# Order of work inside and between the stages of a two-layer language-model tower, on one core

## What is computed

```python
h = tok(x, ...)                                    # embedding rows + position + type, layernorm
h = h + attn0(layernorm(h), Wq, Wk, Wv)            # 32 sequences of 128 tokens, 192 features, causal
h = h + ffn0(layernorm(h), phi, ln_g, ln_b, ...)   # soft mixture: 64 experts x 16 slots, hidden 384
h = h + attn1(layernorm(h), w_qkv, w_proj, b_proj) # 12 heads of 16, rotary tables
h = h + ffn1(layernorm(h), router_w, w1, b1, ...)  # top-1 routing to 8 experts, hidden 768, tanh gelu twice
```

## Time and profile before

| | |
|---|---|
| median of 3 runs | 1349.08 us (1348.38 to 1349.42) |
| the profiled execution | 1348.99 us, span 1347.3 us |
| busy PE / DVE / ACT / POOL | 95% / 73% / 70% / 21% |
| mean granted clock of TensorE | 0.99 of full |

### The profile page before, as it was taken

The page is one execution under the profiler, slowest core; times in us unless marked ns, Lnnn a source line. Parts: engine busy times, 40 slices in busy tenths (PEclk is TensorE's granted clock), DMA queues, the critical chain, the costliest instruction groups (busy, mean ns, idle before and its releaser), DMA issues. The chain is left out here.

```text
span 1347.3 us, 29296 instructions
## 1 busy us (share of the span) xinstructions
PE 1275.2 (95%) x8693; PEld 1139.1 (85%) x8693; DVE 987.0 (73%) x3078; ACT 949.2 (70%) x2393; POOL 286.2 (21%) x317
## 2 busy tenths in 40 slices
PE   8789999999999999999999999799999999969997
PEld 6578888887899998999989998688888888858886
DVE  6988888556787777777777776489999999932331
ACT  2478888888766666666666665288888988845552
POOL 5331110000111111111111110113333233221335
PEclk9999999999999999999999999899999999989999
DMA  6134444447666666666666665655555556315642
GB/s 201 51 136 159 163 167 157 154 179 247 180 199 194 202 191 197 197 194 203 191 195 198 192 203 162 205 148 165 151 167 153 160 161 171 107 40 143 133 97 23
DMA packets 180178, 220.16 MB, mean 163 GB/s; under 512 B 23572, under 2 KB 147002, under 8 KB 180080
## 3 DMA queue, kind: packets, MB, share of 16 engines
q1 hardware_dynamic: 146912, 178.81, 43.6%
q10 hardware_dynamic: 25488, 33.19, 7.3%
q0 software_dynamic: 7680, 6.95, 2.7%
HBM read 141.51 MB, written 79.90 MB: 164 GB/s over the span
## 5 line engine op out<-in xcount | busy, mean ns | idle before, releaser
L1361 PE MATMUL bank<-e_w,e_h_full 128*128 128x192 f32 x1920 | 324.9, 326 | 0.4
L1361 PEld LDWEIGHTS bank<-e_w,e_h_full 128*128 128x128 f32 x1920 | 310.6, 190 | 1.7 <-ACT e_h_full L1442 1.3
L1442 ACT ACTIVATE e_h_full<-bank,e_b 128x512 f32<-128x512 f32 x240 | 165.3, 689 | 154.7 <-PE bank L115 154.7
L1297 POOL TENSOR_TENSOR e_ln_rstd<-e_ln_var_eps,minus_half 128x4 f32<-128x4 f32 x62 | 62.5, 1008 | 436.5 <-DVE e_ln_var_eps L1493 436.5
L1899 ACT ACTIVATE probs<-bank,head_neg_max 128x128 f32<-128x128 f32 x384 | 134.9, 392 | 8.6 <-DVE head_neg_max L2143 7.2
L1500 DVE TENSOR_SCALAR e_rows<-e_slot_sums,e_ln_mean_var,e_ln_rstd 128x192 f32<-128x192 f32 x248 | 77.5, 376 | 77.6 <-POOL e_ln_rstd L1297 77.6
L1403 ACT ACTIVATE e_x_full<-bank,e_ln_shift,e_ln_gain 128x512 f32<-128x512 f32 x124 | 76.5, 667 | 40.9 <-issue 36.6
L1110 PE MATMUL bank<-x,dispatch_weights 128*128 128x193 f32 x512 | 96.0, 329 | 5.9 <-ACT slot_stage L955 4.9
L115 PE MATMUL bank<-e_x_hi,e_w1hi 128*128 128x512 f32 x216 | 95.1, 440 | 4.4 <-DVE e_x_hi_over_lo L109 2.0
L1752 PE MATMUL bank<-slot_outputs_then_w_part,combineT 128*128 128x193 f32 x512 | 94.0, 336 | 1.5 <-ACT combineT L1877 1.5
L1752 PEld LDWEIGHTS bank<-slot_outputs_then_w_part,combineT 128*128 128x128 f32 x512 | 84.7, 192 | 7.7 <-issue 7.2
(11 more groups left out here) (295 smaller groups left out, 3064.5 us busy)
## 6 DMA issues: line engine op xcount, KB each, us to landing
slot_sums<-slot_stage SPq DMA_DIRECT2D x64, 386.0 KB, 3.2
e_slot_sums<-slot_sums SPq DMA_DIRECT2D x64, 386.0 KB, 3.6
slot_outputs<-e_stage ACTq DMA_DIRECT2D x64, 384.0 KB, 3.6
slot_outputs_then_w_part<-slot_outputs SPq DMA_DIRECT2D x30, 768.0 KB, 4.9
e_w<-in_w SPq DMA_DIRECT2D x64, 288.0 KB, 2.9
slot_logits<-kept_logits SPq DMA_DIRECT2D x32, 512.0 KB
slot_logits<-slot_logits SPq DMA_DIRECT2D x32, 512.0 KB, 3.8
e_w1raw<-in_w SPq DMA_DIRECT2D x80, 192.0 KB, 2.7
```

The lines of the kernel that those rows point to most:

```text
L1297: pool.tensor_tensor(rs[u][:], ve[u][:], half[:], ALU.pow).then_inc(rstd_ready, 1)
L1361: last = pe.matmul(y, hf[:, k, js], w2s[u][:, k, :], start=k == 0, stop=k == MT - 1)
L1442: act.activation(hf[:, m, :], hbank(u, m), act_fn, bias=b1s[:, m, ds(n, 1)]).then_inc(acted, 1)
```

## The change

Five parts. (1) Tower: for groups after 3, the first statistics move from slot 0 to slot 6 of the turn before, the mean's subtraction from slot 1 to slot 2, and from group 3 on the type rows are added in slot 5. (2) Combine: the values' product of `q > 0` goes ahead of the transposes of `x4`. (3) Drain: both roundings of the large weights go to the end of ACT's turn 33, both differences to the end of DVE's last turn 36; ACT's router exponentials of turn 33 go behind the batch's own work. (4) Spare products: 6 are added at the start of turn 33, 6 become 2 in turn 34, 4 become 3 ahead of the last head outputs, 20 become 28 at the end, 4 become 7 and 4 become 5 at the seam. (5) Large experts: ACT rounds straight from the banks and DVE subtracts straight from them (no `xf`), the transposes wait for `x_split` in place of `x_taken`; for expert 0 the products of banks 0 and 1 that need only the rounded main part are issued before the split, and the rows of expert 1 are turned after these two banks and taken by ACT after its second gelu.

```diff
@@ tower, DVE
+                AHEAD = 3
                 def embed(e, s):
-                    if s == 0:
+                    if s == 0 and e <= AHEAD:
...
                         norm_stats(e, st6, mv, ve, evar)
-                    if s == 1:
+                    if s == (1 if e <= AHEAD else 2):
                         for j in range(GB):
                             st.did(dve.scalar_tensor_tensor(hrow(e, j), hrow(e, j), mv[:, j, 0:1], T["gamma"][:],
                                                             ALU.subtract, ALU.mult))
+                    if s == 1:
...
-                    if s == 6 and 2 < e + 1 < NG:
+                    if s == (6 if e < AHEAD else 5) and 2 < e + 1 < NG:
                         add_types(e + 1)
+                    if s == 6 and AHEAD < e + 1 < NG:
+                        st.wait_apart()
+                        norm_stats(e + 1, st6, mv, ve, evar)
@@ experts, PE
-                    past(pe, x_taken, 2 * n)
+                    if routed:
+                        past(pe, x_split, n)
+                    else:
+                        past(pe, x_taken, 2 * n)
...
+                        begun = 2 if routed and isinstance(n, int) and n == 0 else 0
+                        pe.wait_ge(w1_split, n + 1)
+                        if begun:
+                            pe.wait_ge(x_hi_ready, 1)
+                            for m in range(begun):
+                                ms = slice(m * P, (m + 1) * P)
+                                pe.matmul(hbank(u, m), w1hi[u][:, 0, ms], xhi[u][:, 0, :], start=True, stop=False)
+                                pe.matmul(hbank(u, m), w1lo[u][:, 0, ms], xhi[u][:, 0, :], start=False, stop=False)
                         pe.wait_ge(x_split, n + 1)
-                        pe.wait_ge(w1_split, n + 1)
-                        for m in range(MT):
+                        for m in range(begun):
...
+                        if begun:
+                            turn_rows(1, 1)
+                        for m in range(begun, MT):
...
-                    keep_busy(pe, T, idle_bank, 4)
+                    keep_busy(pe, T, idle_bank, 7)
                     turn_rows(0, 0)
-                    keep_busy(pe, T, idle_bank, 4)
-                    turn_rows(1, 1)
+                    keep_busy(pe, T, idle_bank, 5)
@@ experts, ACT
+                def round_turned(n, u):
+                    act.wait_ge(turned, 2 * n + 1)
+                    past(act, w1_done, (n - 1) * MT)
+                    act.activation(xhi[u][:, 0, :], bank[:, 0, :], ACT.Copy).then_inc(x_hi_ready, 1)
+                    act.wait_ge(turned, 2 * n + 2)
+                    round_rest(act, xst[u], bank[:, 1, 0:2 * P]).then_inc(x_hi_ready, 1)
...
+                            if routed and isinstance(n, int) and n == 0 and m == 1:
+                                take_x(1, 1)
@@ experts, DVE
                 def split_x(n, u):
+                    if routed:
+                        dve.wait_ge(x_hi_ready, 2 * n + 1)
+                        dve.tensor_tensor(xlo[u][:], bank[:, 0, :], f32(xhi[u][:, 0, :]), ALU.subtract)
+                        dve.wait_ge(x_hi_ready, 2 * n + 2)
+                        less_rounded(dve, xst[u], bank[:, 1, 0:2 * P]).then_inc(x_split, 1)
+                        return
@@ combine, PE
-                    if t >= NB + 2:
-                        keep_busy(pe, T, bank[:, 0, :], 6)
+                    if t > NB:
+                        keep_busy(pe, T, bank[:, 0, :], 2 if t == NB + 2 else 6)
...
+                    if q is not None and q > 0:
+                        past(pe, S["v_took"], q)
+                        heads_of(bank[:, 3, 0:D + NE1], slice(2 * D, 3 * D + NE1), "v_done")
                     if y is not None:
                         pe.wait_ge(S["x4_ready"], y + 1)
                         for k in range(2):
                             last = pe.transpose(x4T[:, k * P:(k + 1) * P], x4[:, k * P:(k + 1) * P], ident[:])
                         last.then_inc(S["x4T_done"], 1)
-                    if q is not None:
+                    if q == 0:
...
-                            keep_busy(pe, T, bank[:, 0, :], 4)
+                            keep_busy(pe, T, bank[:, 0, :], 3)
...
-                keep_busy(pe, T, bank[:, 0, :], 20)
+                keep_busy(pe, T, bank[:, 0, :], 28)
@@ combine, ACT
-                    if z is not None:
...
+                    if z is not None and t != NB + 1:
+                        exp_logits(z)
-                    if t == NB:
-                        large_w1_hi(0)
...
-                    if t == NB:
-                        large_w1_hi(1)
...
+                    if z is not None and t == NB + 1:
+                        exp_logits(z)
+                    if t == NB + 1:
+                        large_w1_hi(0)
+                        large_w1_hi(1)
@@ combine, DVE
-                    if t == NB + 1:
-                        large_w1_lo(1)
...
-                    if t == NB:
+                    if t == NB + 4:
                         large_w1_lo(0)
+                        large_w1_lo(1)
```

More of the change, by code:

```diff
@@ L1338, in turn @@
                         n = i * 2 + u
-                        pe.wait_ge(x_split, n + 1)
-                        pe.wait_ge(w1_split, n + 1)
-                        for m in range(MT):
+                        begun = 2 if routed and isinstance(n, int) and n == 0 else 0
[6 more added lines that the diff above has]
+                                pe.matmul(hbank(u, m), w1lo[u][:, 0, ms], xhi[u][:, 0, :], start=False, stop=False)
+                        pe.wait_ge(x_split, n + 1)
+                        for m in range(begun):
+                            ms = slice(m * P, (m + 1) * P)
+                            pe.matmul(hbank(u, m), w1hi[u][:, 0, ms], xlo[u][:], start=False, stop=False)
+                            pe.matmul(hbank(u, m), w1hi[u][:, 1, ms], xst[u][:], start=False, stop=False)
+                            pe.matmul(hbank(u, m), w1lo[u][:, 1, ms], xst[u][:], start=False, stop=True
+                                      ).then_inc(w1_done, 1)
+                        if begun:
+                            turn_rows(1, 1)
+                        for m in range(begun, MT):
                             past(pe, acted, n * MT + m - 1)
@@ L1393, in w1_hi @@
                     act.activation(w1hi[u][:], w1raw[u][:], ACT.Copy).then_inc(w1_hi_ready, 1)
+                def round_turned(n, u):
[4 more added lines that the diff above has]
+                    round_rest(act, xst[u], bank[:, 1, 0:2 * P]).then_inc(x_hi_ready, 1)
                 def take_x(n, u):
+                    if routed:
+                        round_turned(n, u)
+                        return
                     for k, c in enumerate((4 * P, 2 * P)):
@@ L1399, in take_x @@
                         past(act, x_split, n)
-                        if ln is None:
-                            last = act.activation(xf[:, k, 0:c], bank[:, k, 0:c], ACT.Copy)
-                        else:
-                            last = act.activation(xf[:, k, 0:c], bank[:, k, 0:c], ACT.Identity,
-                                                  bias=lnb[:, k, ds(n, 1)], scale=lng[:, k, ds(n, 1)])
-                        last.then_inc(x_taken, 1)
+                        act.activation(xf[:, k, 0:c], bank[:, k, 0:c], ACT.Identity, bias=lnb[:, k, ds(n, 1)],
+                                       scale=lng[:, k, ds(n, 1)]).then_inc(x_taken, 1)
                     round_x(n, u)
@@ L1461, in _ @@
                     take_x(0, 0)
-                    take_x(1, 1)
                 each_pair(act, turn)
@@ L1820, in turn @@
                         last.then_inc(S["x4T_done"], 1)
-                    if q is not None:
+                    if q == 0:
                         past(pe, S["v_took"], q)
-                        if q == 0:
-                            pe.wait_ge(S["R_split"], 1)
-                            pe.wait_ge(S["WpR_took"], 1)
+                        pe.wait_ge(S["R_split"], 1)
+                        pe.wait_ge(S["WpR_took"], 1)
                         heads_of(bank[:, 3, 0:D + NE1], slice(2 * D, 3 * D + NE1), "v_done")
@@ L1891, in take_values, with exp_logits @@
                                    ).then_inc(S["v_took"], 1)
+                def exp_logits(z):
+                    act.wait_ge(S["logits_read"], z + 1)
+                    act.wait_ge(S["ln5_rstd"], 2 * z + 2)
+                    past(act, S["lex_summed"], z)
+                    for j in range(2):
+                        c = (2 * z + j) % 4
+                        last = act.activation(lex[:, j, :], lx[:, j, :], ACT.Exp, scale=rs5[:, c:c + 1])
+                    last.then_inc(S["router_exped"], 1)
                 def turn(t, u, n, y, q, a, p, r, z, w):
@@ L1902, in turn @@
                         take_values(a, u)
-                    if z is not None:
-                        act.wait_ge(S["logits_read"], z + 1)
```

(10 more changed lines are left out.)

## The result

The changed kernel takes 1331.99 us (median of 4 runs, 1331.64 to 1337.41) against 1349.25 us beside it: ratio 0.9879, 95% interval 0.986 to 0.9899, that is 17 us less with 14 to 19 as bounds. Forecast was 1330.1. The profiled execution took 1332.14 us, its span 1330.4 us.

What follows compares the result with a forecast made beforehand. PE, DVE and ACT are all nearly full in the steady combine, so only small recurring waits can go. Loop 10.2, drain 5.1, seam 2.6 and tower 1.1 sum to 19.0: 1349.1 becomes 1330.1 us, range 1325.5 to 1341.5.

Steps and rivals of the forecast that it cites:

- loop: Combine's turns 2 to 31: the values' product fills PE's wait for x4; 0.34 us in each of 30 turns, 10.2 us.
- drain to the row transposes: After the combine's loop: large-weight work no longer delays scores and projection, and the block ends 5.1 us sooner.
- seam: Start of the large experts: split ready sooner, first products made ahead of it, third bank 2.6 us sooner.
- tower: Tower slots: statistics and subtraction move to where DVE has time; 1.1 us over four turns, bounds 2.5 and -1.
- the combination's other input: Combine turn: ACT's `exp_combine`, waiting for DVE's L1955, limits the gain to 0.34 us, or 0.41 in even turns.
- 14 was far off: Upper bound of the combine loop's gain: 0.47 us a turn, 14 us in all.
- The doubt in the even turns: Combine: DVE's maxima start 1.44 us after the scores in 13 even turns with POOL's second scatter, 1.03 in odd ones.
- the rival in which they rule: Combine's even turns: maxima come 1.43 us after the scatter's start regardless of scores; 4.8 us for 10.2, 1335.4; chance 0.19.
- the fourth rival: Block's end: the last two scatters wait for DVE's differences, costing 3.4 us, 1333.5; chance 0.06.
- the spares miss: Drain and seam: added spare products don't hold the clock, some 30 products lose 0.2 us each, 6 us, 1336; chance 0.07.
- the scatter rival: Combine's even turns: scatter start sets when DVE's maxima come; 13 pairs and 4 free turns give 4.8 us, 1335.4; chance 0.19.
- the third bank: Start of the large experts: PE begins this bank's products at 1215.75 in place of 1218.37, 2.6 us sooner.

Runs made afterwards that it cites:

- loop alone: The kernel before with only the values' product ahead of the x4 transposes in the combine's loop; 1339.28 us, ratio 0.9915.
- drain alone: The kernel before with only the large weights' roundings and differences moved later and the drain's spare products redistributed; 1346.38 us, ratio 0.9974.
- tower alone: The kernel before with only the tower's new slot order; 1346.96 us, ratio 0.9984.
- the repeated kernel: The changed kernel run once more with nothing altered, against the kernel before; 1331.34 us against 1349.02, ratio 0.9874.

## Why the prediction was right, and where it was off

The direction and nearly all mechanisms held. The terms, by the kernels that part them:

| term | forecast | measured | from |
|---|---|---|---|
| loop | 10.2 | 9.9 | loop alone: turns 3 to 30 9.1, turn 31 0.4 up to the row numbers; turn 2 0.4 by the first profiles |
| drain to the row transposes | 5.1 | 3.3 | drain alone |
| seam | 2.6 | 2.7 | with the drain's spares |
| tower | 1.1 | 1.7 | tower alone against its neighbours |
| sum | 19.0 | 17.6 | the repeated kernel: 17.7 by medians, 17.0 by its ratio |

*Loop.* "By PE alone a turn gets 0.47 shorter", and the combination's other input leaves 0.34 or 0.41: the turns are 9.55 and 9.65, so 0.37 and 0.27 were had, a mean of 0.32. What closes the turn isn't what I wrote. In the even turn x4's transposes start 7.12 us into it, as worked out, the inverse sums' at 7.54 and the scores at 7.88, each 0.1 behind the working; in the odd turn the scores at 7.96 are 0.1 behind. From there PE's own order runs on: the next combination starts 0.79 to 0.80 us after the head outputs, in the old order and in the new. ACT's weights, the "other input", are ready 0.12 us before it in both turns (9.43 for 9.55, 9.51 for 9.64), and no wait on them shows, though the prediction expected one. So PE closes the turn, and ACT would have closed it less than 0.1 us sooner: the limit was the wrong one, its size nearly right. 14 was far off.

*The doubt in the even turns.* I wrote that the trace doesn't say why the maxima are late beside the second scatter, and gave the rival in which they rule 0.19. In the first profile the rival's mechanism was there: the maxima started 1.43 us after the scatter and behind the combination. Its price was half the rival's (a pair gained 0.48, not 0.26): the maxima came 0.77 us later than in the repeated kernel and the turn behind them was only 0.15 longer, so DVE had more room in it than I had assumed. In all later profiles the mechanism is absent and the forecast's sum stands. I had taken a regular pattern of 13 turns for a property of the program. It was one of that execution or its chip.

*Drain.* This is the term that was mis-sized. The six spares ahead of the projection did what I took them for: it took 1.70 us in the kernel before, in a stretch at a granted clock of 0.52, 0.94 at 1.00 in the changed kernel, and 1.70 at 0.50 in the kernel with these six and the closing eight taken out. In the kernel with the drain's part alone the steps came out one by one, relative to the start of turn 31: scores 1.38 sooner (forecast 1.45), the projection 3.05 (3.1), head outputs 3.91 (4.25), the following projection 4.79 (5.1), the last products of row numbers 4.68. The 0.3 that go missing at the head outputs lie in ACT's three copies of the probabilities, which end 3.7 sooner and not 3.95. What failed is the step behind: "So I cost the scatters at nothing, with a bound of 2 x 1.7 = 3.4 us." They lost 1.12 us, a third of the bound. This is the fourth rival, at a third of its price.

The timeline shows how. The first difference ends at 1186.05 + 1.75 = 1187.80 and the scatter that began inside it 0.85 later; the second difference ends at 1189.47 and its scatter 0.84 later. A free one takes 0.97. So of a scatter that starts while the difference runs all but 0.12 or 0.13 us of the free time comes after the difference's end, whether 0.86 or 0.52 us of the difference were left at its start. What I hadn't looked at is who starts first: in the earlier trace rows the gather starts at 51.21 and the DVE operation at 51.23, so POOL was first. With 0.02 us between them that row is thin, but the tower has a clearer pair, DVE's addition of the type rows beside a gather. First the repeated changed kernel, where DVE is first, then the changed kernel's first profile, where POOL is:

```profile
10.59 0.96 DVE L678 TENSOR_TENSOR h_all_and_logits<-h_all_and_logits,typed 128x768 f32<-128x768 f32 x1
10.77 1.59 POOL L611 DMA_INDIRECT h_all_and_logits<-in_tok,ids  x1 [0.30 <-issue]
```

```profile
10.78 0.95 POOL L611 DMA_INDIRECT h_all_and_logits<-in_tok,ids  x1 [0.30 <-issue]
10.92 0.96 DVE L678 TENSOR_TENSOR h_all_and_logits<-h_all_and_logits,typed 128x768 f32<-128x768 f32 x1
```

The gather takes 1.59 to 1.60 us in all six profiles in which DVE is 0.18 us ahead, and 0.95 in the two in which POOL is 0.14 ahead. None of these DVE operations is longer for a POOL that was first. The addition takes 0.96 us either way, the operation of the earlier trace rows 1.24 beside the gather and 1.23 with none, and the second difference, which started at 1187.72 with the first scatter still on its way, 1.75 like all the others.

*Seam.* 2.7 for 2.6, and the first product 1.88 us after the rows' transposes for "some 1.8". The old seam took 13.11 to 13.84 us in five profiles and the new one 10.38 to 10.44 in seven, so 2.7 is the low end. What I didn't see is that it leans on the drain's spares. The rival "the spares miss" was priced at 6 us, from 30 products at 0.2 us more each; the 0.2 is read from the earlier trace rows, four products in 1.70 us at 1187.41, in a stretch at a granted clock of 0.52, and in 0.84 at 1195.53. Measured, taking 14 of the 18 added ones out costs 2.1 by the profile and less by the medians, mostly at the seam, where the clock is at 0.50 and the rows are late, not in the drain.

*Tower.* 1.7 for 1.1, inside the bounds. Four turns got shorter, as worked out, but by 0.36 us three times and by 0.7 once, not by 0.27 each.

*The time.* The first profile had 2 us against it from the late completions and some 1.6 us for it ahead of turn 3: its first 14 combination products ran at a clock of 1.00 and those of the kernel before at 0.59. Of the 1.6 none comes from the change, nor do the 2; they nearly cancel in the span. That the first median came within 2 us of the forecast is in part luck: the drain's 1.8 us too many were made up in part by the tower's 0.6 too few. The range, 1325.5 to 1341.5, held both medians with room. (Two sums of the prediction are off in the last digit: the scatter rival's gives 1335.5, and the third bank comes out at 1215.67.)

## What to carry to other kernels

A spare product paid here where PE otherwise idled and the granted clock was low behind it, ahead of work that somebody waits for. At the seam the spares behind 1.8 us of idleness or less ran at a clock of 1.00 in all seven profiles, those behind 2.5 us at 0.54 and 0.50 in two of four, and those behind 2.9 and 3.6 us at 0.50 to 0.54 in all three. The number of spares is set by when the wait ends, not by when the data should come: too few cost 1.4 us on seven products. When a DVE operation as long as the differences (1.75 us) or the addition of the type rows (0.96 us) may lie beside an indirect DMA on POOL, read who starts first in the row you cite: that was 1.59 us or 0.95 for the gather. Work that nobody needs before a barrier can go behind it. And before a regular pattern in one profile becomes a term of a sum, look for it in a second execution; in the same way, a gain of 1 or 2 us that one profile shows may not show in the medians of four runs each.

## What the runs showed of the hardware

- Beside the two differences of the large weights (1.75 us each) the last two scatters on POOL, started with 0.86 to 0.87 and 0.50 to 0.52 us of the difference left, ended 0.84 to 0.86 us after it, in all six profiles in which they lie there: 1.71 to 1.73 and 1.35 to 1.37 us, for 0.97 to 0.99 in the eight others. Beside the addition of the type rows (0.96 us), started 0.18 us into it, the gather ended 0.82 us after it and took 1.59 to 1.60 us for 0.95, in six profiles; started 0.14 us ahead of it, in two, it took 0.95, and DVE's operation 0.96 in both orders. Not every DVE operation beside an indirect DMA does this: the gather at 52 us starts 0.07 us into a product of `typed` (L673), with 0.39 us of it left, and takes 0.94 to 0.95 in all fourteen profiles, while three gathers near 10.7 us, 0.08 to 0.12 us into such a product, take 1.11 to 1.15. What sets them apart no run shows.
- PE's completion of the scores, seen by its semaphore, came 1.34 to 1.40 us after their start in place of 0.94, and 1.65 to 1.72 in the changed kernel, when POOL issued an indirect DMA beside the scores: in all 13 such turns of two profiles and in none of these turns in nine later profiles in which the scatter lay there too. What brings it stays open.
- Seven spare products took 1.83 to 1.86 us after 0.30 to 1.80 us of idleness and 3.22 to 3.33 us after 2.47 to 3.62 us of it; the granted clock over them was 1.00 in the first, 0.50 to 0.54 in the second. Four took 1.16 or 1.17 us at 1.00 after 2.48 us of idleness in two profiles and 2.04 us at 0.50 after 2.47 in a third.
- The first 30 us of the combine differ by up to 5 us between profiles of kernels whose code is the same there: 29.98 us in the one with 6.8 us at a granted clock of 0.50, 35.02 in the one with 17 us. That is larger than any single part of the change but the loop, and a single profiled execution hides it.
